# Raw rows scattered to the experts, later normalised; scatters and batches re-spaced in a fused attention and mixture-of-experts kernel

## What is computed

```python
x = x + conv_ref(_ln_c(x), ...)          # attention: q, k, v, gate, bias, softmax over 128, 4 heads
t = x rows of 128                         # 64 * 128 = 8192 tokens
xf = _ln_t(t)                             # (t - mean) / sqrt(var + 1e-5), per token
gate_logits = xf @ Wg + bg
top_w, top_i = top_k(gate_logits, 2); top_w = softmax(top_w)
out = sum over e of w_dense[:, e] * (gelu(xf @ W1[e] + b1[e]) @ W2[e] + b2[e])
t = t + out
```

## Time and profile before

| | us |
|---|---|
| median of 3 runs | 886.84 |
| lowest, highest | 885.26, 888.75 |
| profiled execution | 883.92 |
| its span | 882.1 |
| start, to the first xs on POOL | 70.9 |
| attention loop, to the last residual | 71 to 492 |
| gap, to PE's first tile | 492 to 575 |
| tile loop, to the last sent row | 575 to 828 |
| final loads, add and store | 828 to 882 |

### The profile page before, as it was taken

One profiled execution on the slowest core, in us unless ns is written; L12 is line 12 of the kernel. 1 busy time (PEld: TensorE's weight loads), 2 busy tenths in 40 slices (PEclk: granted clock), 3 DMA queues, 4 the chain that ended last, 5 costly groups with the idle time before them and its releaser, 6 DMA issues. The chain is left out here.

```text
span 882.1 us, 21328 instructions
## 1 busy us (share of the span) xinstructions
PE 616.5 (70%) x6740; PEld 499.6 (57%) x6740; DVE 646.6 (73%) x2355; ACT 599.6 (68%) x1557; POOL 418.5 (47%) x559
## 2 busy tenths in 40 slices
PE   0066899989977999898887300079999999999100
PEld 0013787777766777676666200068888888887100
DVE  4697688899868888977886386068888888888143
ACT  0374899989977999788886450068787878787100
POOL 4001122212455316455554558627777778777400
PEclk9987799989998899889987555589999999999655
DMA  9974930000000000000000112122323222322499
GB/s 199 225 167 134 133 27 2 2 2 2 18 25 24 13 2 26 23 29 27 25 27 26 37 38 77 46 69 75 86 78 83 78 83 78 84 78 65 104 205 287
DMA packets 61778, 62.02 MB, mean 70 GB/s; under 512 B 20803, under 2 KB 51587, under 8 KB 60006
## 3 DMA queue, kind: packets, MB, share of 16 engines
q1 hardware_dynamic: 51478, 42.38, 22.2%
q0 software_dynamic: 8800, 17.98, 6.2%
q10 hardware_dynamic: 1392, 0.30, 0.3%
HBM read 36.18 MB, written 25.26 MB: 70 GB/s over the span
## 5 line engine op out<-in xcount | busy, mean ns | idle before, releaser
L783 ACT ACTIVATE L<-L,lmin 128x128 f32<-128x128 f32 x512 | 159.6, 399 | 0.2
L700 POOL DMA_INDIRECT expert_out<-yo,rows_all x142 | 139.6, 983 | 41.6 <-issue 21.9
L652 POOL DMA_INDIRECT routed<-pay,pos x128 | 135.9, 1062 | 42.5 <-issue 25.9
L631 POOL TENSOR_TENSOR og<-on,rden 128x256 f32<-128x256 f32 x64 | 39.5, 617 | 184.6 <-DVE on L1002 182.5
L990 DVE CUSTOM_DVE_ANT_0 L<-S,biasN 128x128 f32<-128x128 f32 x512 | 115.0, 284 | 7.4 <-issue 6.8
L1237 DVE SCALAR_TENSOR_TENSOR hl<-hf,hscale,hh 128x512 f16<-128x512 f32 x142 | 106.7, 751 | 5.1
L875 ACT ACTIVATE hf<-S,b_sb,inv_hscale 128x256 f32<-128x256 f32 x214 | 105.0, 568 | 1.4 <-PE S L1440 1.4
L975 DVE TENSOR_TENSOR pl<-PT,ph 128x512 f16<-128x512 f32 x128 | 85.0, 685 | 18.8 <-ACT ph L778 17.9
L1235 DVE TENSOR_SCALAR hh<-hf,hscale 128x512 f16<-128x512 f32 x142 | 69.2, 487 | 36.9 <-ACT hf L875 30.5
L620 POOL TENSOR_TENSOR xs<-x,xs 64x512 fp32r<-64x512 f32 x32 | 40.9, 1279 | 106.5 <-ACT xs L744 81.6
L1455 PE MATMUL PT<-w_h,hh 128*128 x568 | 77.8, 218 | 18.9 <-DVE hl L1237 18.5
(11 more groups left out here) (232 smaller groups left out, 1800.0 us busy)
## 6 DMA issues: line engine op xcount, KB each, us to landing
rows_all<-routed SPq DMA_DIRECT2D x71, 132.0 KB, 1.9
xt<-in_x SPq DMA_DIRECT2D x8, 512.0 KB, 12.6
shared<-in_L_conv_ln_w SPq DMA_DIRECT2D x8, 512.0 KB, 31.3
lnb_all<-in_L_conv_ln_b SPq DMA_DIRECT2D x8, 512.0 KB, 34.7
shared<-expert_out SPq DMA_DIRECT2D x16, 256.0 KB, 11.4
pay<-expert_out SPq DMA_DIRECT2D x16, 256.0 KB, 10.9
out<-xt SPq DMA_DIRECT2D x16, 256.0 KB, 9.1
expert_out<-yo,rows_all POOLq DMA_INDIRECT x142
```

The lines of the kernel that those rows point to most:

```text
L652: pool.indirect_dma_start(routed, bass.IndirectOffsetOnAxis(ap=pos[:, slot, i:i + 1], axis=0), pay[:, i, :], None).then_inc(scattered[slot ...
L700: pool.indirect_dma_start(expert_out, bass.IndirectOffsetOnAxis(ap=row_place[t % IN_BUFS][:, k, W + 1:W + 2], axis=0), yo[t % YO_BUFS][:, ...
L783: last = nc.scalar.activation(L[p][:, h, i, :], L[p][:, h, i, :], ACT.Exp, scale=-1.0, bias=lmin[p][:, h * R + i:h * R + i + 1])
```

## The change

- The rows are sent raw. `xt` becomes the first 128 columns of `pay`, whose two spare columns now hold the row's scale and shift (`rstd_row`, `shift_row`). `normalise_rows` on ACT goes. x is loaded into rows with a stride of 132 floats, and the final store reads from them; one of the two final inputs has a plain buffer `other_half` of its own.
- In the tile loop the loaded rows are normalised in place: DVE takes the first half of tile s + 3 at the end of its step (`normalise_first`), POOL the second half of tile t + 5 where the two memsets stood (`normalise_second`); before the loop DVE does three tiles and POOL five. PE waits for both.
- Batches of 5, 5, 3, 3 groups instead of 3, 4, 3, 3, 3. Six scatters a step: two ahead of `gate` 0, four between the gates, none behind `gate` 1 up to step 35. The batch before the last (`HASTY`) is placed and weighed one step sooner and may be scattered one step sooner. A wait of POOL for `totals_summed` goes.
- The last group's statistics and scales are computed right behind the last residual. `square_weights` moves behind the copy for the last gate logits, `weight_scales` and the sum of squares behind all attention steps, `high_weights` behind the last gate exponential, after one tiny Gelu. DVE's w_l goes in 16 parts instead of 2.

```diff
-    PHASES = ((0, 3), (3, 7), (7, 10), (10, 13), (13, 16))
+    PHASES = ((0, 5), (5, 10), (10, 13), (13, 16))
-    PER_STEP = 5
+    PER_STEP = 6
+    HASTY = len(PHASES) - 2
-                            if step_no > PHASE_READY[k] + 5)
-                done = min(known, done + PER_STEP) if step_no <= LAST + 1 else known
+                            if step_no >= PHASE_READY[k] + (4 if k == HASTY else 5))
+                done = min(known, done + PER_STEP) if step_no <= LAST else known
...
+        xt, rstd_row, shift_row = pay[:, :, 0:W], pay[:, :, W + 2], pay[:, :, W + 3]
...
-                if slot == 0 and i % R == 0:
-                    pool.wait_ge(xn_ready, i // R + 1)
...
-                scatter(range(first + 2, min(first + 4, stop)))
+                scatter(range(first + 2, min(first + 6, stop)))
                 unit(s, p, 2, gate, 1)
-                scatter(range(first + 4, stop))
+                scatter(range(first + 6, stop))
...
+            def normalise_second(t):
+                pool.wait_ge(rows_loaded[t % IN_BUFS], 16 * (t // IN_BUFS + 1))
+                half = rows_in[t % IN_BUFS][:, 1]
+                nc.gpsimd.tensor_scalar(half[:, 0:W], half[:, 0:W], half[:, W + 2:W + 3], half[:, W + 3:W + 4],
+                                        ALU.mult, ALU.add).then_inc(rows_second, 1)
+
             def pause(t):
-                nc.gpsimd.memset(placed[:], 0.0)
-                nc.gpsimd.memset(ranked[:], 0.0).then_inc(paused, 1)
-                pool.wait_ge(paused, t + 1)
+                if t + AHEAD < TILES:
+                    normalise_second(t + AHEAD)
+                    pool.wait_ge(rows_second, t + AHEAD + 1)
+                else:
+                    nc.gpsimd.memset(placed[:], 0.0).then_inc(paused, 1)
+                    pool.wait_ge(paused, t + AHEAD - TILES + 1)
...
+                for part in range(8):
+                    k = slice(part * NQ, (part + 1) * NQ)
+                    last = nc.vector.scalar_tensor_tensor(flat(w_l[n][:])[:, k], raw[:, k], hscale[:, n:n + 1], flat(w_h[n][:])[:, k],
+                                                          ALU.mult, ALU.subtract)
...
+                if s >= 0 and s + 3 < TILES:
+                    normalise_first(s + 3)
```

110 lines of the change are left out of this document (56 added, 54 removed).

## The result

The changed kernel takes 876.3 us (median of 4, 874.5 to 878.9), the kernel before 887.4 on the same chip: ratio 0.989 (95% interval 0.985 to 0.992), 11 us. The forecast was 33 us. Both the missing 22 us and the difference between the chips have to be explained.

The account below looks back on a forecast made before the run. PE and ACT were taken as full in bare attention steps, POOL as the chain in the gap. Terms summed to -33 us from the profiled 883.92, giving 851, median forecast 854; 8-in-10 range 832 to 878.

Parts of the forecast that it names:

- steps 2 to 4: Attention loop: normalising off ACT, fewer batches and rearranged scatters save time; -29.9 us with the last gate's cost.
- step 4: Attention loop: six scatters a step, none behind the second gate, let xs start earlier; -13.5 us, bounds -4 and -22.
- Rival C: Attention loop does not give back what was counted, bare work at a lower clock fills steps; 874 us, chance 0.15.
- rival D: Attention loop: with fewer holes the clock stays up, savings near upper bounds, tile loop stays 3.37; 829 to 835, chance 0.14.
- Step 1: Start: x lands in rows of 132 floats, in shorter pieces, so loading takes longer; +3.3 us, bounds 0 and +5.
- -1 for the memsets: Tile end: the last five tiles have one memset instead of two, where POOL runs last; -1 us.
- Step 2: Attention loop: normalising leaves ACT, 1.1 us for ten groups and 2.5 for the last three; -13.5, bounds -5 and -22.
- Step 3: Attention loop: four batches instead of five save one set of short DVE operations; -5 us, bounds -1 and -8.
- last gate +2.1: Last attention unit: the second gate must wait for four scatters, 5.2 us instead of 3.2 behind the first; +2.1 us.
- Step 5: Gap: 46 scatters instead of 48, placing earlier, w_l in 16 parts holds scatters up less; -14.6, bounds -8 and -18.
- Steps 6 and 7: Tile head: earlier Gelu table offsets DVE's first normalising, 0. Tile loop: DVE and POOL exclude each other, +0.13 a tile, +9.
- Rivals A and B: Tile loop: DVE-POOL exclusion costs more; A 3.7 a tile, 870 us, chance 0.17; B slower than before, 893, chance 0.07.

Follow-up runs that it names:

- before_again: The kernel before, unchanged, run on chip 11: 862.0 us.
- b_six: The kernel before with six scatters a step instead of five, four between the gates and none behind the second; chip 11: 837.6 us, ratio 0.970.
- norm: The changed kernel with the 64 normalising activations put back on ScalarE, written to a tile nobody reads; chip 11: 847.0 us, ratio 0.988.
- after_again: The changed kernel, unchanged, run on chip 11: 844.3 us, ratio 0.977 to the kernel before there.
- none: The changed kernel with all 128 scatters behind the last step of the attention loop; chip 11, one execution: 932.0 us.
- b_wl: The kernel before with the expert weights' low parts made in 16 instructions instead of two; chip 13: 882.2 us, ratio 0.992.
- b_long: The kernel before with six scatters a step, none behind the second gate, and batches 5, 5, 3, 3; chip 13: 904.3 us, ratio 1.017.
- five: The changed kernel with five scatters a step: two, gate 0, two, gate 1, one; chip 11: 856.3 us, ratio 0.993.
- after_third: The changed kernel, unchanged, run on chip 3: 881.6 us, ratio 0.993 to the kernel before.

## Why the prediction was wrong

It forecast the sign of the whole and 33 us where 11 (or 17.7) came. The step that failed is the attention loop, steps 2 to 4 of the sum with the last gate: forecast -29.9, measured +8.2 on the first chip (+0.6 and +7.6) and -10.2 on chip 11 (-15.4 and +5.2). The total is nearer than that by luck: the gap came out 2.6 us better than forecast and the tile loop 13. The 38 us that the loop missed on the first chip fall into two parts.

- 18 of them are the difference between the chips. The sum let a row of four scatters go for nothing except at the last gate; where signals are held such a row delays PE's signals by 2.5 us. This is the overlap in step 4 that the prediction had wrong.
- 20 of them are missing on chip 11 too, where nothing is held. Split by the profiled runs from the second xs to the last gate: before_again to b_six, the scatters' rule, -15.3 where the sum had -11.4 (4 better); b_six to norm, batches and order, +8.3 where it had -5 (13 worse); norm to after_again, normalising, -3.2 where it had -13.5 (10 worse). These are single executions, and medians give the normalising 9, so the last two shares are rough.

Rival C, 874 us, named the outcome: the attention loop does not give back what was counted. The reason that it gave, bare work at a lower clock filling the steps, is not what sets the changed kernel apart on the first chip: the loop there has 72.8 us at half clock against 68.4 before, and PE is busy 331.9 us against 333.6. On chip 11, where fewer waits remain, the half-clock time falls from 58.3 to 48.7 us and PE's busy time by 8.5, which is the direction of rival D. Half-clock stretches do stand in the long steps of the first chip (0.88 in the windows above), and none in the two short ones of chip 11. How much of the 3.1 us of such a step is the wait itself and how much the work at half clock behind it (PE is busy 2.15 us longer in the step at 309.95 than in that at 317.11 of chip 11) is not separated.

**Step 1, start: +3.3.** The first xs is 3.0 us later (2.8 on chip 11). Right. Two more us up to the second xs come and go among kernels with the same start (86.9 to 88.7 us); in the four slower ones, and in none of the others, the granted clock is at half for 3.4 us from 72.4 to 73.7 on. At the end the stores land in 4.2 us instead of 9.1, the two streams of loads in 12.4 and 11.8 instead of 10.9 and 11.4 (medians of the pages); rest +1.1, where the sum had 0 for them and -1 for the memsets.

**Step 2, normalising: -13.5.** Measured 3 to 9 on chip 11 (norm). The mechanism is there and the term was probably too large. Its price of 1.1 a step was not what the row says either: 11.4 less 10.6 is 0.8, with other work in it.

**Step 3, batches: -5.** Not confirmed. On chip 11, from the second xs to the last gate, b_six takes 381.2 us and norm, which differs from it by the batches, the order around them and the rows' layout, 389.5: these cost 8.3 instead of saving 5. The price of 5 a batch was a remainder: 28 bare steps of 10.6 us make 297 us, not 292, which leaves less than 4 a batch. And run none shows that a batch of five groups adds 8 to 10 us, so that fewer and longer batches save little. Of the 8.3 the trace names 6.7: in steps 17 and 27, the first ones with scatters of a batch, POOL waits for the labels. The row is in every trace of a kernel with the changed order and scatters in the loop, and in none of the kernel before, b_wl, b_six or b_long; b_long has these batches in the old order, so it is the order that makes the wait. Here on chip 11, timeline of POOL:

```profile
268.03 1.26 POOL L617 TENSOR_TENSOR xs<-x,xs 64x512 fp32r<-64x512 f32 x1
272.69 0.22 POOL L644 COPY pay<-label 128x40 int32<-128x40 int32 x1 [3.39 <-DVE label L1101]
273.50 1.10 POOL L647 DMA_INDIRECT routed<-pay,pos  x1 [0.60 <-POOL pay L644]
274.91 0.97 POOL L647 DMA_INDIRECT routed<-pay,pos  x1 [0.30 <-issue]
275.89 0.63 POOL L628 TENSOR_TENSOR og<-on,rden 128x256 f32<-128x256 f32 x1
```

The gate behind the copy is 3 us late, its step 14.9 us long. The change lets scatters begin one step sooner after every batch (>= in place of > in scatters_through), not only after the one called HASTY, for which it is two. The prediction read that line for its count of scatters and not for the wait that it puts into POOL's queue, ahead of a gate. No run priced it alone.

**Step 4, scatters: -13.5, last gate +2.1.** This is the step that failed. Where no signal is held its mechanism is right: PE's wait for xs went from 19.7 to 4.1 us in b_six and from 16.7 to 2.4 on the first chip, and the size is 12 to 14 between five and six (five) or -24 in the kernel before (b_six). Wrong on the first chip: the sum took a run of four as free but for the last gate. It holds PE's signals for 2.5 us, 12 times up to the last unit; 18 us is what the change loses there beside chip 11. The trace of before had its sign: one wait of 1.8 us of DVE and one of 1.1 of ACT, "remote", each beside two or three scatters in a row. I had not looked at them. The last units cost more than 2.1 too (+7.6 and +5.2): on the first chip the gates at 489.01 and 499.79 start at once behind a scatter (timeline of POOL):

```profile
497.53 0.98 POOL L647 DMA_INDIRECT routed<-pay,pos  x1 [0.28 <-issue]
498.81 0.95 POOL L647 DMA_INDIRECT routed<-pay,pos  x1 [0.30 <-issue]
499.79 0.63 POOL L628 TENSOR_TENSOR og<-on,rden 128x256 f32<-128x256 f32 x1
```

**Step 5, gap: -14.6.** From the last gate to the last scatter's start it is 65.6 us (499.79 to 565.36), before 82.7: -17.1, forecast -14.6. Right, and b_wl shows that the pieces alone bring 7 to 8 of it.

**Steps 6 and 7, tiles: +9.** The exclusion of DVE and POOL is there, and small. Groups by line of the changed kernel, first chip (columns as in the earlier trace rows):

```profile
L1247 DVE SCALAR_TENSOR_TENSOR hl<-hf,hscale,hh 128x512 f16<-128x512 f32 x142 | 111.1, 783 | 5.1
L1245 DVE TENSOR_SCALAR hh<-hf,hscale 128x512 f16<-128x512 f32 x142 | 68.8, 485 | 16.1 <-ACT hf L867 12.4 <-issue 3.3
L685 POOL TENSOR_SCALAR rows_all<-rows_all 128x128 f32<-128x128 f32 x71 | 35.5, 501 | 23.9 <-ACT yo L875 8.4 <-DMA rows_all<-routed 8.0 <-issue 1.4
```

hl takes 783 ns on the mean, 751 before: 4.5 us in 142. The mean hides two kinds. The second hl of a tile, which runs beside POOL's normalising, takes 818 ns in 67 tiles; the others take 752. So the price is 0.07 us a tile, where I had 0.3. POOL's normalising takes 0.49 beside hl, not 0.3; on chip 11 the nine that meet no hl take 0.44. The hole before hh went from 36.9 us to 16.1, so DVE paid from its slack. The rule of the Trainium skill (SBUF — State Buffer, "Who interferes with whom") has its direction confirmed, at about a quarter of my price.

On chip 11 the tile loop takes 221.6 and 221.9 us with the old tile code (before_again, b_six) and 221.6 to 228.4, on the mean 225.5, in six kernels with the new one: +4 where +9 was forecast. On the chips that hold signals it is no longer than before, 232.9 to 236.9 against 237.0 to 242.8. The 4.1 us gained on the first chip go with fewer late signals: in that loop 26 of them are more than 0.3 us over the usual delay, where the kernel before has 67. after_third, the same program on chip 3, has 70 and takes 236.1. This is a correlation of three traces.

**Rivals A and B** did not come: the period was 3.3 us on the first chip and 3.2 on chip 11, and there is no wait on rows_first or rows_second past the first tile.

## What to carry over

A wait that ends with no instruction ending is a lead, even a single one of 1.8 us: ask how often the change will repeat what stands beside it. When work is moved into a queue in one piece, count how many of the same kind then stand in a row. When its start condition is loosened by a step, look for the producer's end and for what queues behind the wait. And an edit that wins on one chip may win half on the next: compare with the kernel before on the same chip, and before believing a mechanism see whether its mark is in the trace of that chip.

## What the runs showed of the hardware

- Signals of PE's matmuls come late while indirect scatters follow one another on POOL. The usual delay from a matmul's start to its signal is 0.2 to 0.6 us in the attention loop. The longest excess over it beside a row, on the mean of a trace: 0.6 to 1.0 beside pairs, 2.5 to 2.6 beside rows of four (up to 4.1), 2.2 beside three, a gate and three (up to 4.7). The longest-held signal is released 0.8 to 1.0 us after the end of a row of four on POOL, and in the row shown all five within 0.3 us. Only signals of PE were counted; two of DVE and ACT in the row shown (319.81 and 319.91) came in time. What holds them is open.
- It goes with the chip as far as was seen: there on the first (whose number is not recorded) and on 13, 3 and 8, absent on 11 in two sessions, with the same programs. The other chips were visited once each. The kernel before takes 887 to 890 us there and 858 to 862 on chip 11. What differs between them is open.
- 0.76 us of POOL in the middle of a row of four halved the excess of these rows (2.6 to 1.2 us) and gave 12 us, on chip 3; on chip 8 it gave 0.9%.
